# A graph network kernel on one core: the attention product moved next to z, and h turned by two DMA transposes

## What is computed

```python
# first layer, per graph b: x is (c=256, n=512)
q = einsum('c,bcn->bn', wq, x);  k = einsum('c,bcn->bn', wk, x)
scores = leaky_relu(q[:, None, :] + k[:, :, None], 0.01)
att = softmax(scores, axis=-1)                 # 512 x 512
agg = einsum('bcn,bmn->bcm', x, att)
h = layernorm(x + relu(einsum('oc,bcm->bom', adj, agg) + bm))
# second layer: h is (n=256, d=512), mask = adj (256 x 256)
z_l = h @ W_lang.T;  z_g = h @ W_grav.T;  v = h @ W_V.T
A_l = max(cosine(z_l, z_l), 0) * not_eye;  A_g = exp(-dist2(z_g, z_g) / (2 sigma^2)) * not_eye
K = w_l * rownorm(A_l * mask) + (1 - w_l) * rownorm(A_g * mask)
out = layernorm(h + (K @ v) @ W_O.T)
```

## Time and profile before

| | |
|---|---|
| median of 3 runs | 1072.63 us (1071.83 to 1072.81) |
| the profiled execution's own time | 1072.26 us |
| its span, first to last instruction | 1070.3 us |
| busy: TensorE, VectorE, ScalarE, GpSimd | 97%, 82%, 59%, 30% |
| mean granted TensorE clock | 0.994 |
| moved by DMA | 56.33 MB |

### The profile page before, as it was taken

One profiled execution on the slowest core, in us unless ns is written; L12 is line 12 of the kernel. 1 busy time (PEld: TensorE's weight loads), 2 busy tenths in 40 slices (PEclk: granted clock), 3 DMA queues, 4 the chain that ended last, 5 costly groups with the idle time before them and its releaser, 6 DMA issues.

```text
span 1070.3 us, 20032 instructions
## 1 busy us (share of the span) xinstructions
PE 1043.2 (97%) x7429; PEld 723.4 (68%) x7429; DVE 877.3 (82%) x2442; ACT 634.3 (59%) x1203; POOL 325.0 (30%) x280
## 2 busy tenths in 40 slices
PE   7989999999999999999999999999999999999995
PEld 5466767677676766767676676767667676766662
DVE  4767787888889888888988888898888889888767
ACT  2656566485665748566574856657485664748431
POOL 0333315243341524324151432405143240514100
PEclk9999999999999999999999999999999999999998
DMA  7020011030301103030020303002030300202011
GB/s 274 21 77 4 1 64 57 1 119 1 119 1 52 68 1 119 1 119 1 34 87 1 118 2 119 1 26 94 2 118 2 116 5 16 104 2 79 1 40 40
DMA packets 22833, 56.33 MB, mean 53 GB/s; under 512 B 1744, under 2 KB 2256, under 8 KB 20688
## 3 DMA queue, kind: packets, MB, share of 16 engines
q1 hardware_dynamic: 22736, 55.06, 14.1%
HBM read 21.50 MB, written 16.78 MB: 36 GB/s over the span
## 4 chain that ended last, share of the span: by engine, by line
PE 92%; issue 3%; DVE 3%; ACT 1%; POOL 1%; DMA 0%; POOLq 0%; DVEq 0%
PE bank L223 26%; PE bank L224 26%; PE bank L225 26%; PE bank L345 3%; PE bank L428 2%; PE bank L479 2%; PE bank L230 2%; PE bank L259 2%; PE bank L419 1%; PE bank L276 0%; DVE h L1057 0%; POOL y L1129 0%; DMA agg_t<-in_wl 0%; DVE y_stat L1022 0%; ACT y L627 0%
## 5 line engine op out<-in xcount | busy, mean ns | idle before, releaser
L1112 POOL TENSOR_TENSOR att_lo<-att,att_hi 128x512 f16<-128x512 f32 x128 | 157.9, 1245 | 219.8 <-ACT att_hi L532 219.8
L862 DVE SCALAR_TENSOR_TENSOR att<-a_row,u_col,vb 128x512 f32<-128x512 f32 x128 | 126.7, 1010 | 30.3 <-POOL att_lo L1112 30.3
L573 ACT ACTIVATE z_hi<-bank 128x512 f16<-128x512 f32 x128 | 75.7, 591 | 117.1 <-PE bank L225 116.4
L223 PE MATMUL bank<-xw_hi,att_hi 128*128 128x257 f16 x512 | 140.5, 274 | 1.2 <-DVE wvo_lo L746 1.0
L225 PE MATMUL bank<-ht_hi,z_lo 128*128 128x256 f16 x512 | 139.6, 273 | 0.0
L223 PE MATMUL bank<-ht_hi,z_hi 128*128 128x256 f16 x512 | 139.6, 273 | 0.0
L224 PE MATMUL bank<-ht_lo,z_hi 128*128 128x256 f16 x512 | 139.6, 273 | 0.0
L225 PE MATMUL bank<-xw_hi,att_lo 128*128 128x257 f16 x512 | 139.5, 272 | 0.0
L224 PE MATMUL bank<-xw_lo,att_hi 128*128 128x257 f16 x512 | 139.1, 272 | 0.0
L869 DVE TENSOR_TENSOR z_lo<-bank,z_hi 128x512 f16<-128x512 f32 x128 | 87.6, 690 | 39.8 <-ACT z_hi L573 37.7
L634 ACT ACTIVATE xw_hi<-bank 128x256 f16<-128x256 f32 x128 | 49.1, 385 | 107.4 <-PE bank L225 107.4
(11 more groups left out here) (173 smaller groups left out, 2703.4 us busy)
## 6 DMA issues: line engine op xcount, KB each, us to landing
x_in<-in_x SPq DMA_DIRECT2D x16, 1024.0 KB, 5.5
x_res<-x_in SPq DMA_DIRECT2D x16, 1024.0 KB, 5.3
out_y<-o SPq DMA_DIRECT2D x32, 512.0 KB, 3.3
agg_t<-in_wl SPq DMA_DIRECT2D x4, 256.0 KB, 3.6
y<-in_wg SPq DMA_DIRECT2D x1, 1024.0 KB, 9.3
o<-in_wv SPq DMA_DIRECT2D x1, 1024.0 KB, 11.5
h<-in_woT SPq DMA_DIRECT2D x1, 1024.0 KB, 13.7
att<-in_adjT SPq DMA_DIRECT2D x1, 256.0 KB, 4.1
```

The source lines that it names most:

```text
L223: pe.matmul(dst, ah, bh, start=(i == 0 and first), stop=False, skip_group_check=skip)
L573: act.activation(z_hi[:, g, :], bank[g % 4][:], ACT.Copy).then_inc(s["z_hi_done"], 1)
L862: dve.scalar_tensor_tensor(out=att[:, g % 2, :], in0=a_row[:, j, :], scalar=u_col[:, j, n:n + 1], in1=vb[:, g % 2, :], op0=ALU.mult, op1=A ...
L1112: pool.tensor_tensor(att_lo[:, n[0], n[1], :], att[:, g % 2, :], att_hi[:, n[0], n[1], :], ALU.subtract).then_inc(s["att_lo_done"], 1)
```

## The change

TensorE's order in a step becomes: z 0 to 7; the attention products 0 to 7 for pair q; the transposes of agg; t 0 to 3; wx 0 to 2; add_transposed 0 and 1; norm_rows; wx 3 to 5; add_transposed 2; wx 6 and 7; add_transposed 3; v 0 to 2; the transposes of k; k_rows for pair r; v 3; o 0 to 3. The banks of wx, v, o and k_rows change accordingly. The other engines' orders follow. The ring of the attention tiles is interleaved with z_hi and z_lo from the start of the step, and t_rows, ab_rows and uv_columns for the next step stand at the end of a step. The output's statistics come after the first den, its norms after the fourth.

For pairs 1 to 15 h is no longer transposed on TensorE. ScalarE makes h_hi, GpSimd makes h_lo (both in the attention tiles' memory), and SyncE issues two DMA transposes in f16, each 128x2048 elements, into ht_hi and ht_lo, which are now double and laid out tile by tile. TensorE waits for both at the start of a step. The first pair (in `early`) keeps the transposes on TensorE. The scaling of a_l by s_l moves from VectorE to ScalarE (k_scale). h is double, so h no longer waits for the residuals. v shares z's memory, kt that of t, and diag_junk that of vb.

In step 0 k_rows(1) stands after the second z product, and t_rows, ab_rows and uv_columns for pair 1 follow it. After the last step the statistics of the last output come after all its residuals. The diff, cut to the parts named here:

```diff
-        h = sb("h", [2 * OC, N])
-        ht_hi, ht_lo = sb("ht_hi", [DC, 2 * O], F16), sb("ht_lo", [DC, 2 * O], F16)
+        h2 = sb("h", [2, 2 * OC, N])
+        ht2_hi, ht2_lo = sb("ht_hi", [2, 4, DC, P], F16), sb("ht_lo", [2, 4, DC, P], F16)
-        v_hi, v_lo = sb("v_hi", [2 * OC, D], F16), sb("v_lo", [2 * OC, D], F16)
-        diag_junk = sb("diag_junk", [8, P])
+        v_hi, v_lo = z_hi[:, 0:2 * OC, :], z_lo[:, 0:2 * OC, :]
+        diag_junk = vb[:].rearrange("p a (b n) -> p (a b) n", n=P)
-        kt_hi, kt_lo = sb("kt_hi", [2, OC, O], F16), sb("kt_lo", [2, OC, O], F16)
+        kt_hi, kt_lo = t_hi[:, 0:2], t_lo[:, 0:2]
+        h_hi, h_lo = att_hi[:, 0], att_lo[:, 0]
...
+        o_bank = (0, 1, 4, 5)
+        v_bank = (2, 0, 1, 3)
...
+            def store(pair):
+
+                for j in range(2):
+                    sp.wait_ge(s["normed"], 2 * pair + j + 1)
+                    sp.dma_start(out_v[pair, j], o[:, 2 * j:2 * j + 2, :]).then_inc(s["stored"], 16)
+
+            def turn_h(pair):
+
+                hi, lo = ht_of(pair)
+                sp.wait_ge(s["h_hi_done"], 4 * pair)
+                sp.dma_start_transpose(hi.rearrange("p k d n -> p (k d) n"),
+                                       h_hi[:].rearrange("p k n -> p (k n)")).then_inc(s["ht_hi_landed"], 16)
+                sp.wait_ge(s["h_lo_done"], 4 * pair)
+                sp.dma_start_transpose(lo.rearrange("p k d n -> p (k d) n"),
+                                       h_lo[:].rearrange("p k n -> p (k n)")).then_inc(s["ht_lo_landed"], 16)
+
...
+                if p >= 1:
+                    store(p - 1)
+                if p >= 0 and l0:
+                    turn_h(q)
...
+            def step(p, l0, new):
+                if p < 0:
+                    return early(p)
+                q, r = p + 1, p + 2
+                ht_hi, ht_lo = ht_of(p)
+
+                if p > 0:
+                    pe.wait_ge(s["ht_hi_landed"], 16 * p)
+                    pe.wait_ge(s["ht_lo_landed"], 16 * p)
+                for g in range(8):
+                    hi, lo = (ul_hi, ul_lo) if g < 4 else (ug_hi, ug_lo)
+                    e = slice((g % 4) * P, (g % 4 + 1) * P)
+                    if p == 0 and g < 4:
+                        pe.wait_ge(s["ht_lo_done"], g + 1)
+                    if p > 0 and l0 and g == 2:
+                        pe.wait_ge(s["t_done"], 2 * q + 2)
+                    if p > 0 and g < 2:
+                        pe.wait_ge(s["o_done"], 4 * p - 3 + g)
+                    if g >= 4:
+                        pe.wait_ge(s["z_lo_done"], 8 * p + g - 3)
+                    product(bank[g % 4][:], [(hi[:, d, e], lo[:, d, e], ht_hi[:, :, d, :], ht_lo[:, :, d, :])
+                                             for d in range(g % 4 + 1)]).then_inc(s["z_mm"], 1)
+                    if at(p, 0) and g == 1:
+                        k_rows(1)
+
+                if l0:
+                    for k in range(8):
+                        pe.wait_ge(s["att_lo_done"], 8 * q + 4 * (k // NC) + 4)
+                        if k < 4:
+                            pe.wait_ge(s["z_lo_done"], 8 * p + 5 + k)
+                        att_product(q, k)
+
...
+                def v_product(k):
+                    if new and k < 3:
+                        pe.wait_ge(s["xw_lo_done"], 8 * r + 6 + k)
+                    elif l0:
+                        pe.wait_ge(s["relu_done"], 4 * q + v_bank[k] + 1)
...
+                def norm_rows():
+
+                    pe.wait_ge(s["r_l_done"], p + 1)
+                    if l0:
+                        pe.wait_ge(s["relu_done"], 4 * q + 4)
...
+                def wx_product(k):
+
+                    if k % 4 == 0:
+                        pe.wait_ge(s["x_lo_done"], 2 * r + k // 4 + 1)
+                    if k < 3:
+                        pe.wait_ge(s["relu_done"], 4 * q + k + 1)
+                    else:
+                        pe.wait_ge(s["xw_lo_done"], 8 * r + k - 2)
+                    wx_matmuls(p, k)
+
+                if l0:
+                    turn_agg(q)
+                for k in range(4):
+                    t_product(k)
+                if new:
+                    for k in range(3):
                         wx_product(k)
-                if l0:
-
-                    pe.wait_ge(s["h_done"], 4 * q + 4)
-                    for d in range(DC):
-                        for k in range(4):
-                            last = pe.transpose(bank[d][:, k * P:(k + 1) * P], h[:, k, d * P:(d + 1) * P], ident[:])
-                        last.then_inc(s["ht_mm"], 1)
-                if new and not at(p, -2, -1):
+                add_transposed(0)
+                add_transposed(1)
+                norm_rows()
+                if new:
+                    for k in range(3, 6):
                         wx_product(k)
+                else:
+                    v_product(0)
+                add_transposed(2)
+                if new:
+                    wx_product(6)
+                    wx_product(7)
+                add_transposed(3)
+                if new:
+                    v_product(0)
+                v_product(1)
+                v_product(2)
+                turn_k(0)
+                turn_k(1)
+                if new:
+                    pe.wait_ge(s["v_lo_done"], 4 * p + 1)
+                    k_rows(r)
+                v_product(3)
+                for k in range(4):
+                    o_product(k)
...
+                def k_scale():
+
+                    act.wait_ge(s["sl_done"], p + 1)
+                    for k in range(4):
+                        act.activation(a_l[:, k // 2, k % 2, :], a_l[:, k // 2, k % 2, :], ACT.Copy,
+                                       scale=s_l[:, k:k + 1]).then_inc(s["kl_done"], 1)
...
+                def h_hi_tile(k):
+                    act.wait_ge(s["h_done"], 4 * q + k + 1)
+                    act.activation(h_hi[:, k, :], h_of(q)[:, k, :], ACT.Copy).then_inc(s["h_hi_done"], 1)
+
                 if l0:
+                    vb_tile(q, 0)
+                    vb_tile(q, 1)
+                    z_hi_tile(0)
+                    for g in range(8):
+                        att_hi_tile(q, g)
+                        if g < 6:
+                            vb_tile(q, g + 2)
+                        for i, after in enumerate((0, 2, 3, 4, 5, 6)):
+                            if g == after:
+                                z_hi_tile(i + 1)
+                    z_hi_tile(7)
                     for k in range(8):
+                        agg_tile(q, k)
+                        if new and k in (1, 3):
+                            x_hi_tile(k // 2)
+                    for k in range(4):
+                        relu_tile(q, k)
+                t_hi_tile(0)
+                t_hi_tile(1)
                 if l0:
-                    wait(act, s["h_done"], 4 * q)
+                    h_hi_tile(0)
+                    h_hi_tile(1)
+                t_hi_tile(2)
                 if l0:
-                    for d in range(DC):
-                        act.wait_ge(s["ht_mm"], 4 * q + d + 1)
-                        act.activation(ht_hi[:, d, :], bank[d][:], ACT.Copy).then_inc(s["ht_hi_done"], 1)
-                if new and not at(p, -1):
-                    for k in range(4, 8):
-                        xw_hi_tile(k)
+                    h_hi_tile(2)
+                    h_hi_tile(3)
+                t_hi_tile(3)
+                if new:
+                    for k in range(3):
+                        xw_hi_tile(p, k)
+                if new:
+                    for k in range(3, 6):
+                        xw_hi_tile(p, k)
+                else:
+                    v_hi_tile(0)
+                exp_tile(0)
+                if new:
+                    for k in range(6, 8):
+                        xw_hi_tile(p, k)
+                exp_tile(1)
+                if new:
+                    v_hi_tile(0)
+                k_scale()
+                v_hi_tile(1)
+                v_hi_tile(2)
+                for j in range(2):
+                    act.wait_ge(s["kt_mm"], 2 * p + j + 1)
+                    act.activation(kt_hi[:, j], halves[4 + j], ACT.Copy).then_inc(s["kt_hi_done"], 1)
+                v_hi_tile(3)
+                if new:
+                    ab_rows(r)
+                    uv_columns(r)
...
                 if l0:
-                    for d in range(DC):
-                        dve.wait_ge(s["ht_hi_done"], 4 * q + d + 1)
-                        dve.tensor_tensor(ht_lo[:, d, :], bank[d][:], ht_hi[:, d, :], ALU.subtract)\
-                           .then_inc(s["ht_lo_done"], 1)
+                    for g in range(8):
+                        att_tile(q, g)
+                        for i, after in enumerate((0, 1, 3, 4, 5, 6, 7)):
+                            if g == after:
+                                z_lo_tile(i)
+                    z_lo_tile(7)
+                    den(q, 0)
+                    o_stats()
+                    den(q, 1)
```

(73 more changed lines are left out.)

898 lines of the change are left out of this document (420 added, 478 removed).

## The result

The kernel before takes 1072.34 us (median of 4 runs), the changed one 1138.98 us (4 runs, 1137.84 to 1140.47). The ratio is 1.0622, with a 95% interval of 1.0604 to 1.0641. The forecast was 1065 us, so sign and size are both wrong.

What follows compares the result with a forecast made beforehand. TensorE's own work was taken to bound the kernel. From 1072.3 us, 29.8 gained (26.3 of it transposes, the rest waits) against 22.6 lost leaves 7.2 off: forecast 1065 us, range 1052 to 1091.

Steps and rivals of the forecast that it cites:

- rival 3: Slow DMA transposes of h: at 20 us each TensorE waits in 15 steps, 1300 us; chance 0.03.
- rival 4: Not described in the prediction as given, which says only that its worst lies outside 1052 to 1091; no chance stated.
- The 6.0 us of step 0: First step: k_rows(1) stands behind z product 1, att tiles start 7.6 us later, z waits; 6.0 us lost.
- The wait for kt_lo: TensorE's 1.7 us wait in the last step of the kernel before; 1.3 us of it was taken off.
- product 5: Attention product 5 waits for agg tile 1, since den 1 queues behind o_stats on VectorE: 0.2 us lost a step.
- my own sign of being wrong: The prediction is wrong if a place other than agg_t before product 5, xw_lo 3 or step 0's z_lo stops TensorE every step.
- turning agg loses another 0.1: TensorE's transposes of agg, after the attention products, wait behind agg 7: 0.1 us lost a step.
- Rival 2: VectorE late before the attention products, its SBUF reads slowed by GpSimd: 2 us more in 13 steps, 1091 us; chance 0.22.
- the att window: Stretch where VectorE makes att tiles during z's 13 us, at 1.75 us a tile; all hold, about 1 us to spare.
- The wx waits: TensorE waits for xw_lo 3, which VectorE makes only after the masked rows: 0.7 us lost a step.
- my 61.9: Length of a steady step in us: 62.67 less 1.75 for the transposes plus 1.0 of waits.
- the ends of the pipeline: Losses outside the steady steps: 6.0 and 0.8 us in step 0, 0.9 in step 14, 1.9 after the last step.

## Why the prediction was wrong

**What held.** 26.3 us of transposes left TensorE (x7429 to x7189). The DMA transposes were hidden, as taken. Their rows among the DMA issues of the changed kernel (count, us to landing), and SyncE's issue of two:

```profile
ht_hi<-att_hi SPq DMA_TRANSPOSE x15, 4.4
ht_lo<-att_lo SPq DMA_TRANSPOSE x15, 4.7
...
461.73 3.00 SPq L211 DMA_TRANSPOSE ht_hi<-att_hi  x1
464.77 2.06 SPq L214 DMA_TRANSPOSE ht_lo<-att_lo  x1
```

4.4 and 4.7 us are within my 3 to 10, and TensorE never waits for them. So rival 3 (1300 us) is out. So is rival 4: z's matmuls, which read ht in four pieces, still follow each other by 0.216 us (starts at 419.27, 419.48 and 419.70). The 6.0 us of step 0 are 5.9 in the row for z_lo. The wait for kt_lo (1.7) went entirely, of which I had taken 1.3. Waits came at the places named, before product 5 and in wx. But by my own sign of being wrong the prediction fails: a fourth place, the turn, stops TensorE in every step.

**The step that failed** is "turning agg loses another 0.1". It measured 2.73 us in 13 steps, 34 us more in all. The sum took o_norm at its old duration (it gave it no row and no term), though in the new order it lies beside GpSimd's x_lo. Rival 2 named the right engine, o_norm and a late agg 7, but priced it as a rate ("half again as long"), from att's pairs, which average an untouched tile with one that stood. The trace of the kernel before, taken apart, already had it:

```profile
475.28 1.56 DVE L862 SCALAR_TENSOR_TENSOR att<-a_row,u_col,vb 128x512 f32<-128x512 f32 x1 [1.12 <-POOL att_lo L1112]
...
476.77 0.74 DVE L862 SCALAR_TENSOR_TENSOR att<-a_row,u_col,vb 128x512 f32<-128x512 f32 x1
...
475.14 1.16 POOL L1112 TENSOR_TENSOR att_lo<-att,att_hi 128x512 f16<-128x512 f32 x1
```

The pair of 2.23 us is one att tile of 1.56, which starts beside an att_lo and ends 0.54 after it (476.84 and 476.30), and one of 0.74 that meets none. The price of a block is what is left of GpSimd's instruction, 2.3 us for a tile of 1024 columns, not a share of VectorE's own time. The place that rival 2 put first, the att window, held: att has a mean of 1.08 us, and TensorE never waits for att_lo.

**The term that was missing** is the clock: I followed waits and took the work behind them at full speed. 1.6 us after 11 of 13 turns is 18 us.

**Mis-sized.** Product 5 was 0.2 us and measured 0.60. The wx waits were 0.7 and measured 1.13, in two places, 0.62 before wx 3 and 0.51 before wx 6; h 2 and 3 (2.09 instead of 1.00), t_lo 2 (1.55 instead of 0.69) and neg_gs (1.25) lie beside h_lo and are the same block again. It adds up: 2.6 for the turn, 1.4 for the clock, 0.4 and 0.4 for the others and 1.0 of gaps are 5.8 of the 6.0 us by which the step missed my 61.9, and 0.1 is that the mean step before is 62.76 and not 62.67. 13 times 6.0 is 78 us, and the forecast missed by 74, so the ends of the pipeline cost a little less than the sum took. The range ended at 1091 because its upper end was rival 2 at the wrong price.

## What to carry to other kernels

When a change puts a VectorE tensor_scalar from SBUF to SBUF, or a VectorE instruction with two SBUF inputs, beside a GpSimd one (bn_stats and reads of PSUM weren't touched here), price it as a stand of up to one whole GpSimd instruction, however small the VectorE one is, and look who is queued behind it. The cures are to order the two so that they take turns (46 of the 67 us here), or to cut GpSimd's instruction (30). An even pair in a trace ("x2, 2.23") should be taken apart before its mean is used. And a cause that seems to be worth nothing when taken away alone (3 us) may be worth 40 once the queue beside it is mended.

## What the runs showed of the hardware

- A GpSimd tensor_tensor and VectorE's f32 tensor_scalar take turns: 2.35 us beside a 2.29 us instruction, 1.37 beside 1.32, 0.55 alone; even two columns stand, 1.0 to 1.2 us. So do VectorE's instructions with two SBUF inputs: tensor_tensor (y_add, 1.89 instead of 0.69) and scalar_tensor_tensor (att, 1.56 instead of 0.74).
- A wait of 2.7 us in otherwise unbroken TensorE work brought the granted clock down at 11 of 13 and 11 of 14 turns in two kernels, one of 1.6 us at none of 13, one of 0.9 at none of 14. Each fall cost about 1.6 us.
- A DMA transpose of 128x2048 elements from SBUF to SBUF lands in 4.3 to 4.7 us (medians), and its issue takes SyncE 1.3 to 3.4 us. The Trainium skill ("VectorE: DVE Perf Modes", the three transpose paths) gives 1309 ns for one 128x128 block by DMA, which I had estimated at 21 us for 16 blocks in a row. The trace doesn't agree with that estimate: the whole transpose lands in 4.3 to 4.7 us.
